# Graph attention 2: the aggregate as three 16-bit products, the attention sums read from the PSUM banks

## What is computed

```python
def gat_conv(x, ei, W, a_src, a_dst, bias, heads, out_ch, concat):
    xl = (x @ W).reshape(n, heads, out_ch)
    e = leaky_relu((xl * a_src).sum(-1)[src] + (xl * a_dst).sum(-1)[dst], 0.2)
    e = exp(e - segment_max(e, dst)[dst])
    alpha = e / (segment_sum(e, dst)[dst] + 1e-16)
    out = segment_sum(xl[src] * alpha[:, :, None], dst)      # concat for 4 heads, mean for 1
    return out + bias

h  = relu(layer_norm(gat_conv(norm(x), ..., heads=4, out_ch=256))) + (norm(x) @ Wr1 + br1)   # graph attention 1
h1 = h
h  = layer_norm(gat_conv(h1, ..., heads=1, out_ch=768)) + (h1 @ Wr2 + br2)                   # graph attention 2
x  = x + h
# then a transformer block on 625 tokens: layer norm, 12-head causal attention, projection,
# layer norm, router with one expert of 8 per token, two expert products
```

## Time and profile before

| | us |
|---|---|
| median of 3 runs | 1100.09 |
| lowest and highest of them | 1097.21, 1101.49 |
| the profiled execution | 1102.97 |
| its span | 1101.2 |

### The profile page before, as it was taken

One profiled execution on the slowest core, in us unless ns is written; L12 is line 12 of the kernel. 1 busy time (PEld: TensorE's weight loads), 2 busy tenths in 40 slices (PEclk: granted clock), 3 DMA queues, 4 the chain that ended last, 5 costly groups with the idle time before them and its releaser, 6 DMA issues.

```text
span 1101.2 us, 19073 instructions
## 1 busy us (share of the span) xinstructions
PE 1037.7 (94%) x6167; PEld 651.7 (59%) x6168; DVE 729.8 (66%) x1300; ACT 570.8 (52%) x782; POOL 184.9 (17%) x186
## 2 busy tenths in 40 slices
PE   5999999999999999989998699999999999999997
PEld 3555558756766775566777255555555555555554
DVE  6677768595666654189976888911129898989411
ACT  2666769513240344178834576811128778777310
POOL 3000040040205331072001301110103120211000
PEclk9999999999999999989998699999999999999999
DMA  8300030301507500030026699940009999999100
GB/s 312 106 0 0 1 115 1 115 1 59 112 1 156 87 1 1 1 112 2 2 86 201 244 390 325 351 168 0 25 0 352 375 375 360 390 359 390 72 4 3
DMA packets 92263, 155.60 MB, mean 141 GB/s; under 512 B 36507, under 2 KB 36587, under 8 KB 92214
## 3 DMA queue, kind: packets, MB, share of 16 engines
q1 hardware_dynamic: 89814, 149.20, 39.2%
q0 software_dynamic: 2400, 5.77, 1.5%
HBM read 153.21 MB, written 7.77 MB: 146 GB/s over the span
## 4 chain that ended last, share of the span: by engine, by line
PE 75%; DVE 10%; issue 5%; ACT 4%; DMA 2%; POOL 1%; DVEq 1%; SPq 0%; ACTq 0%; POOLq 0%
PE psum L1519 29%; PE psum L1794 18%; PE psum L1769 17%; PE psum L1778 2%; PE psum L1507 2%; PE psum L1557 2%; DVE area L1380 2%; DMA low<-in_L_ffn_W_dram 2%; DVE smalls L1021 1%; PE psum L1765 1%; PE psum L1677 1%; DVE area L1351 1%; DVE area L1108 1%; ACT low L915 1%; PE psum L1621 1%
## 5 line engine op out<-in xcount | busy, mean ns | idle before, releaser
L1380 DVE TENSOR_TENSOR area<-low,area 128x1536 f16<-128x1536 f32 x144 | 245.9, 1753 | 13.3 <-ACT area L970 13.1
L1519 PE MATMUL psum<-area,low 128*125 128x512 f16 (+4 forms) x1068 | 236.9, 381 | 1.3 <-DVE low L1253 1.3
L1769 PE MATMUL psum<-area,low 128*128 128x512 f16 x972 | 220.7, 381 | 0.0
L1794 PE MATMUL psum<-area,low 128*128 128x384 f16 x1296 | 219.3, 327 | 0.0
L970 ACT ACTIVATE area<-low 128x1536 f16<-128x1536 f32 x138 | 200.3, 1484 | 34.0 <-DMA low<-in_L_ffn_W_dram 28.1
L1519 PE MATMUL psum<-area 125*128 125x64 f16 (+10 forms) x1452 | 196.1, 289 | 10.1 <-DVE area L1351 5.5
L1519 PEld LDWEIGHTS psum<-area,low 128*125 128x125 f16 (+2 forms) x1068 | 136.4, 141 | 92.4 <-issue 53.1
L1794 PEld LDWEIGHTS psum<-area,low 128*128 128x128 f16 x1296 | 127.3, 98 | 80.7 <-issue 1.7
L1519 PEld LDWEIGHTS psum<-area 125*128 125x128 f16 (+3 forms) x1452 | 126.7, 122 | 62.8 <-issue 12.3
L1769 PEld LDWEIGHTS psum<-area,low 128*128 128x128 f16 x972 | 95.5, 98 | 113.9 <-issue 3.0
L981 ACT ACTIVATE low<-psum 128x512 f32<-128x512 f32 x54 | 31.9, 591 | 161.5 <-PE psum L1769 158.1
(11 more groups left out here) (246 smaller groups left out, 1183.9 us busy)
## 6 DMA issues: line engine op xcount, KB each, us to landing
low<-in_L_ffn_W_dram SPq DMA_DIRECT2D x144, 768.0 KB, 7.7
area<-in_L_gnn_W_dram SPq DMA_DIRECT2D x2, 3072.0 KB, 11.9
area<-in_L_gnn_Wr_dram SPq DMA_DIRECT2D x2, 3072.0 KB, 15.7
low<-in_x_dram SPq DMA_DIRECT2D x10, 336.0 KB
area<-in_L_ffn_Wv_dram SPq DMA_DIRECT2D x6, 384.0 KB, 6.2
area<-in_L_ffn_Wq_dram SPq DMA_DIRECT2D x6, 384.0 KB, 7.1
area<-in_L_ffn_Wk_dram SPq DMA_DIRECT2D x6, 384.0 KB, 6.1
area<-in_L_ffn_Wp_dram SPq DMA_DIRECT2D x2, 1152.0 KB, 6.7
```

Of the source, the lines that this page charges most:

```text
L1380: dve.tensor_tensor(low_, raw_view(u), high_, ALU.subtract).then_inc(low_ok, 1)
L1519: ins = pe.matmul(place(name)[0:parts, at:at + w], left(q), right(q)[:, at:at + w], start=(q == 0), stop=(q == k - 1))
L1769: ins = pe.matmul(psum[:, (c % 2) * BANK:(c % 2 + 1) * BANK], ht[x_][:, k, :], w1_s[c][w_][:, k, :], start=False, stop=(k == KD - 1 and x_ ...
L1794: ins = pe.matmul(psum[:, (4 + q) * BANK:(4 + q) * BANK + D // 2], hidT[c % 2][x_][:, j, :], w2_s[c][w_][:, j, q * D // 2:(q + 1) * D // 2 ...
```

## The change

`xl2` now goes to SBUF as two 16-bit parts. ACT writes the high part (`xl2[0]`) and no longer counts the slot as emptied. DVE's new `second_values(t)` has three instructions, all of which read the PSUM banks of `xl2` t: the low part (`xl2[1]`), and the two attention sums. After them it counts the slot as emptied, so in the list of items `xl2` goes from "A" to "D", and with it `probT` of layer 2: there ACT writes the transposed probabilities' high part, and a new DVE instruction the low part. The aggregate of layer 2 is 15 16-bit products of 512 columns and 15 of 256 (high by high, high by low, low by high for each of five node tiles). DVE's order around the transformed nodes is new, and the wait for `arows2_in` stands ahead of `second_values(0)`. Layer 1 is as before.

```diff
@@ item_plan
                 if t >= 1:
-                    plan.append((("xl2", t - 1), "A"))
+                    plan.append((("xl2", t - 1), "D"))
...
             if 1 <= i <= n:
-                plan.append((("probT", layer, i - 1), "A"))
+                plan.append((("probT", layer, i - 1), "AD"[layer - 1]))
@@ scalar engine
-                emptied_by(("xl2", t), act.activation(xl2[:, t, :], place(("xl2", t), D, P), ACT.Copy, scale=1.0 / SCALE_UP))
+                act.activation(xl2[0][:, t, :], place(("xl2", t), D, P), ACT.Copy, scale=1.0 / SCALE_UP).then_inc(xl2_high, 1)
...
+                            done(act, ("probT", layer, i - 2))
+                            act.activation(probT2[i % 2][0], tview(("probT", layer, i - 2), T, P, P),
+                                           ACT.Copy).then_inc(prob_high, 1)
@@ vector engine
+            def second_values(t):
+
+                dve.wait_ge(xl2_high, t + 1)
+                product_ = place(("xl2", t), D, P)
+                dve.scalar_tensor_tensor(out=xl2[1][:, t, :], in0=product_, scalar=1.0 / SCALE_UP, in1=xl2[0][:, t, :],
+                                         op0=ALU.mult, op1=ALU.subtract)
+                for q, (row, a, sign) in enumerate(zip(row_a2, (a_src, a_dst), (1.0, -1.0))):
+                    junk = TW + q * D
+                    ins = dve.tensor_tensor_reduce(low[0:P, junk:junk + D], product_, row, sign / SCALE_UP, 0.0, ALU.mult,
+                                                   ALU.add, a[:, t, 0:1])
+                emptied_by(("xl2", t), ins)
+                was_emptied(dve, ("xl2", t))
...
+                    if layer == 2 and 2 <= i < n_ + 2:
+                        dve.wait_ge(prob_high, i - 1)
+                        emptied_by(("probT", 2, i - 2), dve.tensor_tensor(
+                            probT2[i % 2][1], tview(("probT", 2, i - 2), T, P, P), probT2[i % 2][0], ALU.subtract))
...
-            for t in (1, 2):
-                h1T_low(t)
-            graph_low(3, wr2_parts)
-            for t in range(3, T):
-                h1T_low(t)
+            h1T_low(1)
             dve.wait_ge(arows2_in, 32)
             for t in range(T):
-                attention_values(2, t, 1, D, xl2, row_a2)
+                if 1 <= t < T - 1:
+                    h1T_low(t + 1)
+                second_values(t)
+                if t == 1:
+                    graph_low(3, wr2_parts)
@@ matrix engine
-                        product(("agg", layer, i - 2), T, lambda k: probT[i % 2][:, k, :],
-                                lambda k: xl[:, k, h * width:(h + 1) * width], width, P)
+                        if layer == 1:
+                            product(("agg", layer, i - 2), T, lambda k: probT[i % 2][:, k, :],
+                                    lambda k: xl[:, k, h * width:(h + 1) * width], width, P)
+                        else:
+                            product(("agg", layer, i - 2), 3 * T, lambda k: probT2[i % 2][PARTS[k % 3][0]][:, k // 3, :],
+                                    lambda k: xl[PARTS[k % 3][1]][:, k // 3, :], width, P)
```

More of the change, by code:

```diff
@@ L170, in gnn_moe_kernel @@
         distance = A(2, 4125, NP // 2, P).bitcast(F16)
-        xl1, xl2 = v3(A(4, 0, T * HC, P), T), v3(A(4, 0, T * D, P), T)
+        xl1 = v3(A(4, 0, T * HC, P), T)
+        xl2 = [v3(A(4, 0, T * D, P).bitcast(F16), T)[:, :, q * D:(q + 1) * D] for q in range(2)]
+        probT2 = [[v3(A(3, 4096 + (2 * i + q) * 320, 320, P).bitcast(F16)[:, 0:T * 128], T)[:, :, 0:P] for q in range(2)]
+                  for i in range(2)]
         src_row = [A(4, T * HC, N, P), A(3, 4096 + 2 * N, N, P)]
@@ L350, in gnn_moe_kernel @@
         w_high, w_low = sem("w_high"), sem("w_low")
+        xl2_high, prob_high = sem("xl2_high"), sem("prob_high")
         h1_high, hT_high, hT_low, OT_high = sem("h1_high"), sem("hT_high"), sem("hT_low"), sem("OT_high")
@@ L823, in probT_copy @@
                             done(act, ("agg", layer, i - 4))
-                        copy(("probT", layer, i - 2), probT[i % 2], tview(("probT", layer, i - 2), T, P, P))
+                        if layer == 1:
+                            copy(("probT", layer, i - 2), probT[i % 2], tview(("probT", layer, i - 2), T, P, P))
+                        else:
+                            done(act, ("probT", layer, i - 2))
+                            act.activation(probT2[i % 2][0], tview(("probT", layer, i - 2), T, P, P),
+                                           ACT.Copy).then_inc(prob_high, 1)
                     def source_row(h):
```

## The result

The changed kernel takes 1110.96 us (median of 5 runs, 1108.34 to 1112.5) against 1101.49 us for the kernel before (1097.21 to 1102.83): the ratio is 1.0092, with a 95% interval from 1.0076 to 1.0109. It is slower by 8.4 to 12.0 us, about 10.1 us. The profiled execution took 1108.34 us, with a span of 1106.6.

The account below looks back on a forecast made before the run. PE was taken to bound the stretch; a 12.0 us longer stretch up to xl2 3, less 3.2 us net from the aggregates, gave +8.8 us on the median 1100.09, so 1108.9 us, with an 8-in-10 range of 1104.0 to 1113.0.

Parts of the forecast that it names:

- The landing of the rows: DMA queue: the attention rows land last, at 280.7 us, so DVE starts second_values(0) at 281.3.
- The gap: PE ahead of xl2 2: it stands still for 9.8 us, until 285.4, waiting for DVE's h1T_low 2.
- The slow clock: PE's xl2 2 behind its idle time: half clock at first makes the product 2.1 us longer.
- graph_low(3): DVE ahead of h1T_low 3: xl2 3 possible at 295.9 by DVE, 296.2 by PE; 2.0 us hold if rows are early.
- The aggregates: PE, layer 2: 4.87 us a tile instead of 6.45; PE 4.8 us ahead at res2 2 after waits for low parts.
- The norm chain: DVE and POOL up to res2 4: PE waits there nearly 3 us; of 4.8 us ahead, 3.2 are left.
- The rows landing with POOL's: Rival at the DMA queue: attention rows in by 275.4, PE waits 3.9 us, time 1103.0 us; 6%.
- the wait that doesn't bind: Rival at DVE's wait for the rows: xl2 2 starts as before, graph_low(3) holds xl2 3, time 1098.9 us; 7%.
- The slow side: Rival on PE and DVE: clock cost twice 2.1 us, or dearer low parts and sums, time 1112.7 us; 10%.
- PE runs without a gap from QT on: PE behind the stretch: no gap from QT on, nothing changes there, so the shift stays to the end.

Follow-up runs that it names:

- e1: Changed kernel with the DMAs of a_src2 and a_dst2 issued ahead of the other four rows; 0.9996 of the kernel before, stretch 150.43 us.
- e2: Changed kernel with the two attention rows issued third and fourth of six instead of last; 1.0040 of the kernel before, stretch 154.91 us.
- e3: Changed kernel with graph_low(3) behind h1T_low 3 instead of ahead, attention rows still last; 1.0079 of the kernel before, stretch 159.56 us.
- e4: Changed kernel with the attention rows issued first and graph_low(3) behind h1T_low 3; 0.9978 of the kernel before, stretch 148.38 us.
- e11: Changed kernel with DVE's norms in another order, residual sums ahead of the previous tile's first norm; 1.0069 of the kernel before, stretch 158.24 us.
- e7: Changed kernel with attention rows first, graph_low(3) later, Wv's low part at step 2, and layer 2's low-by-high aggregate product left out; 0.9910 of the kernel before.

## Why the prediction was right

**The landing of the rows** was the term on which the sign hung, and it held. 281.3 was forecast from the bytes moved and POOL's wake-up; it was 281.17. e1 and e2 show that the place in the queue sets it.

**The gap** was forecast at 9.8 us and was 9.59. **The slow clock** was forecast at 2.1 us; xl2 2 took 9.54 instead of 7.96, 1.58 us more. So xl2 3 started 294.45 − 257.02 = 37.4 us behind xl2 0, for 284.08 − 258.06 = 26.0 before. Up to there the stretch grew by 11.4 us, where the working had 12.0. The clock is the term that was too large, and it carries 0.5 of the 0.7 us between 8.8 and 8.1. The row that it was priced by stood behind two gaps: 7.43 us, and then, behind 1.7 us of PE's work, 3.64 us more, as this line of the kernel before shows:

```profile
618.26 0.61 PE L1765 MATMUL psum<-low 112*128 112x512 f16 x1 [3.64 <-DVE low L1401]
```


**graph_low(3)** was said to be covered by the slow clock to within 0.3 us. e3 gives 0.27 us, most of it a product that ran faster, e4 against e1 gives 2.05 us once nothing covers it (1.83 us of it stand in e1's trace as a wait), for 2.0 in the working.

**The aggregates**: 15 pairs take 329.49 to 334.4, 4.9 us, as forecast from xl2's pairs. The wait of aggregate 0 grew from 0.39 to 1.24 us (by 0.8 in the working), and aggregate 1 waited 1.65 us (2.0 in the working). Aggregate 2 had none, where 0.4 was forecast: low part 2 took 0.79 us and came just in time. Until res2 2 PE gained 4.8 us in the working: it starts 100.66 us behind xl2 0, for 94.16 before, so of the 11.4 us 6.5 are left, and the gain is 4.9.

**The norm chain** was said to give back 1.6 us, all at res2 4, with a wait of nearly 3 us there. The sum was right: 8.08 − 6.50 = 1.58 us. The net gain of this part was 11.4 − 8.1 = 3.3 us, for 3.2 in the working, whose own times (360.4 less 357.1) give 3.3 too. The place was half wrong. PE waited 1.58 us ahead of V 0, which takes the slot of res2 2, and 1.32 us ahead of res2 4. The working had followed only the one wait that the trace of before showed and had not counted four items back for V 0.

**The rivals.** The rows landing with POOL's would have given 1103.0, and the wait that doesn't bind 1098.9. e1 is the second of these made on purpose: 1098.8 were to be expected by its stretch, and it measured 1100.23 beside 1100.06 for the kernel before. The slow side (a clock cost of twice 2.1 us) didn't come with this gap, though e2's 2.63 us shows that the term was less sure than one row made it look.

The time itself, 1110.96 us, is 2.1 us above the forecast of 1108.9. The kernel before measured 1101.49 in the same comparison, 1.4 us more than the median that the forecast started from; the rest isn't placed. (The 1.77 us outside the span are in every execution, 1.7 to 2.2 us of them, so they are no part of what the profiled execution before lay above its median.) The sum also took it that PE runs without a gap from QT on. It doesn't: in the kernel before it waits there 7.4 us for a DMA and 3.6 us for DVE, to name the longest two, so a shift of the stretch need not reach the end unchanged. That the forecast came so close in the whole time is therefore partly luck; in the stretch it was earned, 8.1 us for 8.8.

## What to carry to other kernels

A wait that is moved forward in an in-order queue is priced by when its data lands, even if the trace of before shows nobody waiting for it: count the bytes on the DMA queue up to the last one, and look what is queued behind the waiting instruction. The place of one wait cost far more here than the work moved onto DVE; putting the two small transfers ahead of four others repaid 9.4 us. When two delays end together, test them together: moving graph_low(3) was worth 0.3 us alone and 2.05 us once the other was gone.

## What the runs showed of the hardware that was not expected

A shorter gap cost more clock than a longer one. Behind PE's gap of 9.6 us the product of 7.96 us took 1.58 us longer (1.39 in e3 and 1.51 in e11, behind gaps of 9.66 and 9.71 us), behind that of 3.64 us it took 2.63 us longer, in the one execution that has such a gap (e2). In both the clock fell while PE still stood, to a mean of 0.64 over the long gap and 0.78 over the short one; behind the long gap it came back earlier in the product:

```profile
274.40:284.10 9.70, 0.14 (x2) 0.00 (x0) 3.93 (x7) 1.14 (x2) 1.68 (x1) 0.64 0.17 70
284.10:286.00 1.90, 1.87 (x5) 1.08 (x6) 1.90 (x4) 0.00 (x0) 0.00 (x0) 0.50 0.00 0
286.00:288.00 2.00, 2.00 (x8) 1.17 (x7) 1.97 (x3) 0.00 (x0) 0.00 (x0) 0.69 0.00 0
288.00:290.00 2.00, 2.00 (x11) 1.24 (x10) 2.00 (x1) 0.00 (x0) 0.00 (x0) 1.00 0.00 0
```

Read as stretches at 0.50 and at 1.00, the 0.69 from 286 to 288 is 1.2 us at half clock, so PE worked at half clock for 3.1 us from 284.13 on. In e2 the 0.68 from 282 to 285 is 1.9 us, which makes 5.2 us from 278.69 on. Half of each is the loss, 1.55 and 2.6 us, as the products show. Behind the gap of 2.74 us in e7 V 0 lost 1.7 us. Behind the 1.83 us wait of e1 the clock stayed at 1.00 in the profile's windows. What sets the moment at which it comes back isn't shown.

DVE's normalisation of 768 fp32 values took 0.63 to 0.68 us alone and 2.06 to 2.17 us beside POOL's additions in SBUF, in every trace, the kernel before included; no run moved POOL's additions away. The two of them beside POOL's two additions thus cost DVE about 3 us on the chain that PE waits for (2.14 + 2.16 less twice 0.65).
